# Attention scores and row maxima as float32r products of two parts, with four heads in four 32-row tiles of TensorE

## The reference, cut to what matters

```python
def _L0_xattn_ref(q, k, v, Wq, Wk, Wv, Wo):          # q: 16 x 256 x 128, k = v: 16 x 1601 x 128
    qh = jnp.einsum('bnd,hde->bhne', q, Wq)           # 16 heads of 8
    kh = jnp.einsum('bmd,hde->bhme', k, Wk)
    vh = jnp.einsum('bmd,hde->bhme', v, Wv)
    scores = jnp.einsum('bhne,bhme->bhnm', qh, kh) * SCALE
    att = jax.nn.softmax(scores, axis=-1)
    out_h = jnp.einsum('bhnm,bhme->bhne', att, vh)
    ...
x = x + jnp.tanh(g_xattn[0]) * _L0_xattn_ref(_layernorm(x), ctx_1024, ctx_1024, ...)
x = x + jnp.tanh(g_ffn[0]) * _L0_ffn_ref(_layernorm(x), ...)   # 8 experts, the best 2 of each token
```

## Time and profile before

| what | value |
|---|---|
| median of 3 runs | 1312.21 us (1311.06 to 1314.4) |
| the profiled execution, its time | 1307.59 us |
| its span, first to last instruction | 1305.8 us |
| granted TensorE clock, mean over the span | 0.978 |
| PE busy | 1246.9 us, 95% |
| DVE busy | 1128.7 us, 86% |
| ACT busy | 1083.2 us, 83% |
| POOL busy | 544.3 us, 42% |

### The profile page before, as it was taken

One profiled execution on the slowest core, in us unless ns is written; L12 is line 12 of the kernel. 1 busy time (PEld: TensorE's weight loads), 2 busy tenths in 40 slices (PEclk: granted clock), 3 DMA queues, 4 the chain that ended last, 5 costly groups with the idle time before them and its releaser, 6 DMA issues.

```text
span 1305.8 us, 42169 instructions
## 1 busy us (share of the span) xinstructions
PE 1246.9 (95%) x16217; PEld 619.5 (47%) x16217; DVE 1128.7 (86%) x2076; ACT 1083.2 (83%) x2190; POOL 544.3 (42%) x1208
## 2 busy tenths in 40 slices
PE   4799999999999999999999999999999999999992
PEld 1243444444444444444444444444444444399992
DVE  7897999999999999999999999999999899355444
ACT  2587998989999999999999899999999898866661
POOL 3222435262627262626353544434353512146441
PEclk7798999999999999999999999999999999999996
DMA  3232121212121213121212222222211110288896
GB/s 94 83 91 83 48 72 51 76 47 77 50 79 45 85 38 91 32 70 54 73 55 69 59 64 66 61 67 57 73 51 45 49 45 7 75 268 246 258 273 231
DMA packets 61092, 112.94 MB, mean 86 GB/s; under 512 B 13052, under 2 KB 36476, under 8 KB 60748
## 3 DMA queue, kind: packets, MB, share of 16 engines
q1 hardware_dynamic: 54043, 97.67, 25.6%
q0 software_dynamic: 4320, 8.99, 2.0%
q10 hardware_dynamic: 2529, 3.58, 0.8%
HBM read 52.77 MB, written 13.71 MB: 51 GB/s over the span
## 4 chain that ended last, share of the span: by engine, by line
PE 81%; SPq 6%; DVE 5%; POOL 4%; issue 2%; DMA 2%; ACT 1%; POOLq 0%; DVEq 0%; ACTq 0%
PE pv L841 31%; PE st L783 17%; PE mxp L806 13%; PE st L763 7%; PE st L1057 5%; PE mxp L1067 5%; SPq L403 4%; DVE mx L1567 3%; POOL kf L631 1%; DVE x_sb L1765 1%; POOL ksp L636 1%; PE mxp L813 1%; PE st L919 1%; PE st L871 1%; POOL rows L694 1%
## 5 line engine op out<-in xcount | busy, mean ns | idle before, releaser
L1567 DVE TENSOR_REDUCE mx<-mxp 128x2 f32<-128x1024 f32 x768 | 914.3, 1216 | 43.7 <-PE mxp L806 37.9
L1096 ACT ACTIVATE arena<-st 128x512 f32<-128x512 f32 (+1 forms) x1664 | 884.5, 597 | 72.1 <-PE st L783 60.6
L841 PE MATMUL pv<-arena 128*32 128x256 f32 x6656 | 533.7, 392 | 0.5 <-ACT pv_sb L1103 0.3
L783 PE MATMUL st<-qpack,kpack 51*128 51x256 bf16 (+1 forms) x3328 | 484.7, 274 | 4.2 <-DMA qpack<-mxT 3.1
L806 PE MATMUL mxp<-kpack,qpack 48*128 48x512 bf16 x1536 | 416.1, 390 | 9.1 <-DVE mx L1567 8.9
L783 PEld LDWEIGHTS st<-qpack,kpack 51*128 51x128 bf16 (+1 forms) x3328 | 193.3, 96 | 278.8 <-ACT arena L1096 148.3
L841 PEld LDWEIGHTS pv<-arena 128*32 128x32 f32 x6656 | 131.5, 108 | 174.0 <-issue 109.0
L661 POOL CAST mxs<-nmx 128x8 bf16<-128x8 f32 x64 | 12.4, 194 | 397.3 <-DVE nmx L1578 397.1
L806 PEld LDWEIGHTS mxp<-kpack,qpack 48*128 48x128 bf16 x1536 | 120.9, 94 | 96.1 <-issue 46.2
L1237 ACT ACTIVATE arena<-st,bias 128x256 f32<-128x256 f32 (+1 forms) x172 | 75.0, 438 | 45.9 <-PE st L1057 41.4
L694 POOL DMA_INDIRECT rows<-xrow,pos x64 | 66.1, 1033 | 92.0 <-DVE pos L1422 77.0
(11 more groups left out here) (197 smaller groups left out, 952.9 us busy)
## 6 DMA issues: line engine op xcount, KB each, us to landing
kpack<-ksp SPq DMA_DIRECT2D x750, 50.0 KB
arena<-in_w12T SPq DMA_DIRECT2D x43, 576.0 KB
arena<-in_ctxT SPq DMA_DIRECT2D x15, 800.5 KB, 4.6
qpack<-qsp SPq DMA_DIRECT2D x187, 32.0 KB
xblk<-rows SPq DMA_DIRECT2D x28, 132.0 KB, 4.3
rows<-in_pads SPq DMA_DIRECT2D x8, 264.0 KB
arena<-results SPq DMA_DIRECT2D x8, 256.0 KB, 6.8
arena<-results ACTq DMA_DIRECT2D x8, 256.0 KB, 7.3
```

The lines of the kernel that those rows point to most:

```text
L783: ins = eng.matmul(ring[i][0:n, jj * N:(jj + 1) * N], kpack[rows, b % 2, g * JJ + jj, kt * P:kt * P + n], qpack[rows, b % 2, g * JJ + jj, ...
L841: ins = eng.matmul(pv[32 * j:32 * j + 32, 0:N], vaug[0:n, b % 2, kt, at:at + 32], pt[0:n, (2 * u + rg) % PT_BUFS, jj * N:(jj + 1) * N], st ...
L1096: eng.activation(pt[0:n, c % PT_BUFS, :], ring[bank_of["S", u, p]][0:n, :], ACT.Exp, scale=SCALE).then_inc(s_exp, 1)
L1567: eng.tensor_reduce(mx[:, tj, w, :], src[:, :, 0:WIN], AX.X, ALU.max).then_inc(s_red, 1)
```

## The change

Keys and queries are split into two parts instead of three: the part that float32r holds, and the rest in float32r. Three products of parts are stacked (high x high, high x low, low x high): 24 rows, with the maxima's three rows 27. Packed rows are 4 bytes wide and no longer 2. All matmuls of scores and of windows take float32r operands. A head now has a 32-row tile of its own (`tile_position=(32 r, 0)`), four heads in four tiles.

A step of the scores is still four products of 256 columns, but it covers two heads (a side) for two units: steps 2k and 2k+1 make sides 0 and 1 of units 2k and 2k+1. The weighted values of either unit wait for all four exponentials of the pair. A window takes two heads, a side, and `plan_windows` lays out the order so that the windows of a step come first from the side that its scores don't use. A group has 14 windows now: for each side six of 512 keys and one of 66. The split has two operations in place of four (and in the first batch one in place of three on VectorE). The other tables are new too, by a unit or a few each.

```diff
-K_KIND, Q_KIND = (0, 1, 0, 1, 2, 0), (0, 0, 1, 1, 0, 2)
+K_KIND, Q_KIND = (0, 0, 1), (0, 1, 0)
...
-FIRST, LEAD = 17, 22
+FIRST, LEAD = 19, 25
-WINDOWS_AT = ("0111111121010111101011111110111110110111101111111101",
-              "0000100001000000010001000010000010010000100000000001")
+WINDOWS_AT = ("1120111010111111111101111112111011111101111101211101",
+              "0010001010000000000100000001001000000010000100000100")
...
+            side = min(range(SIDES), key=lambda i: (not left[i], load[i], -len(left[i])))
+            load[side] += 1
+            plan.append(left[side].pop(0))
...
-        kpack = sb("kpack", [P, 2, NP, MP], BF16)
+        kpack = sb("kpack", [P, 2, NG, MP])
...
+            def scores(s, p):
+
+                pair, side = divmod(s, SIDES)
+                r, i = side * SIDE + p, bank_of["S", s, p]
+                rows = slice(r * RSTEP, r * RSTEP + SCORE_ROWS)
                 eng.wait_ge(*freed[i])
...
+                for par in range(2):
+                    u = 2 * pair + par
...
+                    ins = eng.matmul(ring[i][0:n, par * N:(par + 1) * N],
+                                     kpack[rows, b % 2, g, kt * P:kt * P + n].bitcast(F32R),
+                                     qpack[rows, b % 2, g, :].bitcast(F32R),
+                                     start=True, stop=True, tile_position=(r * RSTEP, 0))
+                ins.then_inc(s_st[r], 1)
...
+                for p in range(SIDE):
+                    r, dst = side * SIDE + p, mxp[n % MX_BUFS]
+                    rows = slice(r * RSTEP, r * RSTEP + MAXROW)
+                    if w < NF:
+                        ins = eng.matmul(dst[:, p, 0:WIN],
+                                         qpack[rows, b % 2, g, t * P:(t + 1) * P].bitcast(F32R),
+                                         kpack[rows, b % 2, g, w * WIN:(w + 1) * WIN].bitcast(F32R),
+                                         start=True, stop=True, tile_position=(r * RSTEP, 0))
...
-                eng.wait_ge(s_exp, 2 * u + 2)
+                eng.wait_ge(s_exp, HG * (u // 2 + 1))
...
-                eng.activation(pt[0:n, c % PT_BUFS, :], ring[bank_of["S", u, p]][0:n, :], ACT.Exp,
+                eng.activation(pt[:, c % PT_BUFS, :], ring[bank_of["S", u, p]][:, :], ACT.Exp,
```

More of the change, by code:

```diff
@@ L9 @@
 F32 = mybir.dt.float32
+F32R = mybir.dt.float32r
 BF16 = mybir.dt.bfloat16
@@ L332, in build @@
         st = [ps(f"st{i}", [P, BLK]) for i in range(ST_BUFS)]
[L333 removed]
+        mxp = [ps(f"mxp{i}", [P, SIDE, BLK]) for i in range(MX_BUFS)]
         pv = ps("pv", [P, BLK])
@@ L416, in first_packs @@
                 if K_KIND[part] == 0:
-                    pack_key_rows(eng, 0, 0, part, rg)
+                    for r in tiles:
+                        first_key_rows(eng, 0, part, r)
             eng.wait_ge(s_k3, NK)
@@ L999, in _ @@
                 b, r = divmod(u, UNITS)
-                scores(u, 0, windows(u, 0)[:1])
-                scores(u, 1, [])
-                for w in windows(u, 0)[1:]:
-                    maximum(*w)
+                for p in range(SIDE):
+                    scores(u, p)
+                for n in windows(u, 0):
+                    maximum(n)
                 if u >= LAG:
@@ L1033, in _ @@
                     count_tokens(0)
-                for w in windows(u, 1):
-                    maximum(*w)
+                for n in windows(u, 1):
+                    maximum(n)
             def turn_in(i):
```

390 lines of the change are left out of this document (193 added, 197 removed).

## The result

The changed kernel takes **1910.68 us** (median of 4 runs, 1900.08 to 1933.37) where the kernel before takes 1313.31: 1.4525 times as long, 95% interval 1.4468 to 1.4581 (the ratio leaves out the run of 1933.37, which was over 1.5% slower than the fastest of this kernel). The forecast was 1279. The profiled execution took 1910.42 us with a span of 1908.6; before it was 1305.8. So 603 us have to be found, against a forecast gain of 33.

A forecast was written before the change was run, and what follows sets the result against it. TensorE was taken as the bound, VectorE 5.6% behind. A batch falls from 67.9 to 65.9 us, 32 us over 16 batches, plus 0.8 at the start: 1307.6 to 1274.8 profiled, 1279 as median; range 1253 to 1318.

The forecast's parts named there:

- 12 DMAs a batch and not 48, of the same bytes: Key-row copies and later maxima: nothing on the path; uncovered, 1.5 us a group, 6 a batch.
- at full granted clock: Profile before, 100 to 1080 us: engine busy times were read at full granted clock; no clock loss was priced.
- 0.43 us a block forecast: TensorE's scores-and-window block with one window: 0.33 us in four tiles, 0.10 more for the load; before 0.54.
- half pace: TensorE rival: float32r at half pace, or four tiles running only two at a time; 1429 us, chance 0.12.
- four passes: TensorE rival: float32r products take four passes, 31.2 us more a batch; 1811 us, chance 0.03.
- loads one after another: TensorE rival: a block's six weight loads follow each other, 26.4 us more a batch; 1734 us, chance 0.03.
- rival of new waits: The pair's wait and later maxima take 2 us a batch, spending the gain; 1312 us, chance 0.06.
- TensorE needs 67.9 - 9.9 + 5.2 = 63.2 us: TensorE's need a batch: 67.9 before, less 9.9 by four tiles, plus 5.2 for weight loads at 0.10 a block.
- the saving by the tiles, forecast 9.9: TensorE's score and window blocks in four tiles: 28.1 us a batch before, 18.2 after, 9.9 less.
- clear at 1.0 us a unit: ScalarE's exponentials: 0.50 us each, 1.0 us a unit, 52 a batch; not the bound.
- VectorE as the next bound: VectorE's need of 64.1 us a batch, just above TensorE's 63.2, makes it the bound after the change.
- I expect a batch in 65.9: Batch time with two buffers between TensorE and VectorE: waits for windows go nearly whole, 2.0 us less than 67.9.

The follow-up runs named there:

- e1: Changed kernel with the rows of the three parts interleaved, so each key copy goes to every third row of its tile: 1535.98 us.
- e2: Changed kernel with the maxima's four small DMAs of a group issued by ScalarE on its own queue: 2137.36 us in one run.
- e4: e1 with the low key parts packed at unit 20, not 26, and a group's maxima in three copies, not four: 1582.64 us, ratio 1.1965.
- e12: e7 with the key copies of group 2 issued behind the maxima, and the maxima in three copies: 1416.35 us, ratio 1.0659.
- experiment 5: Changed kernel with 48 key copies of 50 KB a batch and a semaphore for each group, in two runs: e7 1518.15 us, e8 1553.01 us.
- e10: e6 with one stop of TensorE added a batch, a wait for a tiny copy at unit 25: 1369.40 us in one run.
- e9: e7 with one stop of TensorE added a batch, a wait for a tiny copy at unit 25: 1467.98 us in one run.
- e14: e12 with VectorE's long reductions over half of each window's columns, TensorE's work unchanged: 1377.44 us in one run.
- e13: e6 with VectorE's long reductions over half of each window's columns, TensorE's work unchanged: 1283.47 us in one run.
- e6: e4 with the two parts as bfloat16 instead of float32r, in the same four tiles: 1334.26 us, ratio 1.0086.
- e8: Changed kernel with 48 key copies of 50 KB a batch, a semaphore for each group, rows still neighbouring: 1553.01 us in one run.
- e7: Changed kernel with 48 key copies of 50 KB a batch, a semaphore for each group, and interleaved rows: 1518.15 us, ratio 1.1453.

## Why the prediction was wrong

*The DMAs: the step that failed.* The forecast put "12 DMAs a batch and not 48, of the same bytes" and the maxima under "Nothing on the path; uncovered it would be 1.5 us a group, 6 a batch". It counted issues and bytes. Measured, the same bytes stop TensorE for 23 to 25 us a batch. Two things make it: the rows of a copy are neighbours, so that copies of 200 KB move at 60 to 69 GB/s instead of 127 (shown alone in 1: 307 of 366 us of stops); and the maxima, 12 KB, stand behind them, in the engines as well as in the queue (2, 4; with less ahead of them, in e12, their waits are 12 us in all). A third is argued: one semaphore for all groups makes the first window of the next batch wait for the last key row. Those waits, 27 us in experiment 1, are 1.6 in experiment 5, which has a semaphore for each group, but also 1.6 in experiment 4, which keeps the one semaphore and packs the low parts earlier. The key copies of before are small and issued one by one, so the trace that the forecast rested on held no price for copies four times as large.

*The clock: absent from the forecast.* It took "at full granted clock" for given. The half clock cost some 190 us: 237 left by the stops, less 16 x 2.7 for the batch itself (start and experts are within this remainder). Every stop of over 4 us in the attention has half clock in it or right behind it, in all runs, and shorter ones often have; how long it lasts stays open. Neither the length of the stop nor the products behind it decide it alone: e4 shows 3 to 58 us for stops of 5 to 7 us at one place of the order. Whether float32r has a part in it stays open too: outside the last batch, bfloat16 had at most 3.4 us with an added stop of 1.8 (e10), and float32r had once 30.7 with one of 1.82 at another place (e9).

*TensorE's block: right where nothing is in the way.* Four tiles side by side, float32r at the pace of bfloat16, 0.43 us a block forecast and 0.44 measured, the load in the open 0.10 us forecast and 0.105 measured between the shortest blocks (0.435 and 0.330), 0.07 on the mean. The rivals of half pace, of four passes and of loads one after another are all refuted, though the time of each of them came nearer to the result than 1279: none had the key copies in it. (The rival of new waits had the later maxima, but at 2 us a batch, and for the pair's wait too; for the maxima alone TensorE waited 273 us.) In blocks with a window of the last keys, the scores and a full window the shortest is 0.621 us with float32r (e14) and 0.567 with bfloat16 (e13), so the difference doesn't grow with the columns.

*The sum over a batch: mis-sized.* This term would have made the forecast wrong without the DMAs. "TensorE needs 67.9 - 9.9 + 5.2 = 63.2 us" measured 69.0 (e14). The loads were 3.8; the saving by the tiles, forecast 9.9, is at most 67.9 - 65.1 = 2.8. The forecast multiplied the shortest block by the number of blocks. Blocks with one window average 0.50 us even with VectorE light (before: 0.55, shortest 0.54), because their products wait in the midst of the block; in e13 over half of the score loads' idle time (111.8 of 198.8 us) is a wait for ScalarE's exponentials, whose engine the forecast took for clear at 1.0 us a unit. But the earlier trace rows has the same share before, 135.5 of 253.3, so that ScalarE is this limit is only argued, and no run tested it.

*VectorE as the next bound: half right.* That it takes time from TensorE is shown (lightened, it gives back 2.7 us a batch from e6 to e13 and 1.7 from e12 to e14). "I expect a batch in 65.9" is not: with 64.4 us of VectorE and 65.1 of TensorE the batch takes 67.8. Neither is full; with two window buffers each waits for the other in turn, as I read it: more buffers were not tried.

*Start.* 0.8 us earlier was forecast; even in e12 the first batch began 2 us later and took 25 us longer.

What of the 603 us: 366 stops, 43 the batch without stops (16 x 2.7), and some 190 that are not parted further, half clock above all. With nearly all of the stops taken out (e12) the change is still 6.6% slower, and at full clock 70.6 us a batch against 67.9, so the forecast would have had the wrong sign without the DMAs too.

## What to carry to other kernels

Price a merged copy by its destination rows, its packet size and by what is queued behind it, in the engines as well as in the queue; the same bytes in fewer copies are not the same transfer. When an engine gains on one that stands 5% behind it, the shortest block is no price for the mean: read how blocks are spread, and who is waited for inside them. And ask of every new wait on TensorE what it does to the granted clock, since the slow time behind a stop can be longer than the stop, and differ from batch to batch.

## What the runs showed of the hardware

- A float32r product of 256 columns streams in 0.11 us, like bfloat16, where float32 took 0.43 (the blocks differ by one load, 0.435 and 0.330 us, and by no more where they have more columns); its weight load of 128 columns takes 183 ns at full clock in e12, against 94 for bfloat16 in e6.
- Four row tiles run side by side though the engine's order has the products of one tile one behind the other: in the changed kernel products start in all four within 0.02 us (841.90 to 841.92).
- 200 KB copies to eight neighbouring rows: 60 to 69 GB/s; to every third of 24 rows: 127 GB/s. Copies of 50 KB in packets of 3202 bytes, issued 0.7 us apart in before: no difference (177 ns a packet). Copies of 50 KB in packets of 6404 bytes: 458 ns a packet to neighbouring rows (e8), 259 to every third (e7).
- Copies of 3 KB on a queue of their own moved 12 us behind their issue while eight copies of 200 KB to neighbouring rows were under way on another (e2).
- A wait of 2.4 us was followed by 47.8 us at 1.2 GHz in e1, waits of 1.8 us by 0 to 6.8 us in most batches of e9 and by 30.7 in one, and waits of 5 to 7 us at one place of e4 went with 3 to 58 us, in kernels with the same products.
